# A memset in front of each gather of the first graph, and marks, reset rows and carried columns of the second graph moved from VectorE to ScalarE

## What is computed

```python
# first graph: 200,000 edges, sorted by dst
xn  = layernorm(x)
x   = x + relu(xn @ W + segment_sum((xn @ M)[src], dst))
# second graph: 131,072 edges, not sorted, plus one loop per node
h   = (xf @ W_gat).reshape(M, HEADS, NUM_EXPERTS)      # xf = layernorm(x)
e   = leaky_relu(a_src[src] + a_dst[dst], 0.2)
ee  = exp(e - segment_max(e, dst)[dst])
agg = segment_sum(h[src] * (ee / denom[dst])[:, :, None], dst)
scores = layernorm(agg).reshape(M, HEADS, NUM_EXPERTS).mean(1)
# two best experts per row, softmax weights w
out = sum over experts of  w[expert] * (gelu(xf @ W1 + b1) @ W2 + b2)
return x + out
```

## Time and profile before

| | |
|---|---|
| median of 3 runs | 3527.27 us (3522.12 to 3535.72) |
| the profiled execution | 3540.27 us |
| its span, first to last instruction | 3539.0 us |
| mean granted TensorE clock over the span | 0.882 |
| busy: TensorE / its weight loads | 2560.6 us (72%) / 1708.4 us (48%) |
| busy: VectorE | 2344.6 us (66%) |
| busy: ScalarE | 920.5 us (26%) |
| busy: POOL | 2377.0 us (67%) |
| mean DMA rate | 170 GB/s |

### The profile page before, as it was taken

How to read it: one execution, slowest core, us unless ns; L and a number is a source line. 1 busy time by engine, 2 the same in 40 slices (tenths; PEclk the granted TensorE clock), 3 DMA queues, 4 the chain that set the end, 5 groups by cost and what they waited for, 6 DMA issues and landing times.

```text
span 3539.0 us, 36336 instructions
## 1 busy us (share of the span) xinstructions
PE 2560.6 (72%) x10290; PEld 1708.4 (48%) x10315; DVE 2344.6 (66%) x5820; ACT 920.5 (26%) x1581; POOL 2377.0 (67%) x2827
## 2 busy tenths in 40 slices
PE   2556777767677777768877887777798787777725
PEld 1334555545555545546555555555554444443314
DVE  6677676776775555565545555555358898899957
ACT  3000111111112222211111111111145565555514
POOL 3666666666656666646666666666788888888841
PEclk9776998989888989889989888989799999999968
DMA  9676566666666666646666666666622122241147
GB/s 287 227 251 205 180 201 186 204 190 196 203 184 194 205 188 204 201 145 211 202 210 196 200 202 213 197 207 207 171 62 55 45 60 57 55 131 43 41 148 230
DMA packets 476775, 600.78 MB, mean 170 GB/s; under 512 B 72486, under 2 KB 415390, under 8 KB 474526
## 3 DMA queue, kind: packets, MB, share of 16 engines
q1 hardware_dynamic: 378766, 375.94, 32.9%
q0 software_dynamic: 97216, 219.88, 22.4%
q10 hardware_dynamic: 592, 2.64, 0.2%
HBM read 313.06 MB, written 286.79 MB: 169 GB/s over the span
## 4 chain that ended last, share of the span: by engine, by line
DVE 28%; PE 22%; another core or an unknown queue 12%; issue 9%; DMA 3%; ACT 2%; POOL 1%; SPq 0%; DVEq 0%; ACTq 0%; POOLq 0%
PE wide L1535 8%; DVE picked L901 6%; DVE g L905 6%; DVE ring L855 5%; PE wide L1585 4%; PE wide L1595 4%; PE wide L1645 3%; DVE one_hot L788 2%; DMA ring<-xn_d,srci 2%; PE wide L1554 1%; DVE by_row L996 1%; DVE by_row L1003 1%; POOL ring L1737 1%; DVE comb L1178 1%
## 5 line engine op out<-in xcount | busy, mean ns | idle before, releaser
L1737 POOL DMA_INDIRECT ring<-xn_d,srci x1611 | 1562.1, 970 | 907.6 <-issue 415.4
L855 DVE SCALAR_TENSOR_TENSOR ring<-ring,same_v,wide 128x256 f32<-128x256 f32 x1610 | 771.2, 479 | 930.7 <-remote 404.3
L1535 PE MATMUL wide<-ring,one_hot 128*128 128x256 f32 x3222 | 959.1, 435 | 381.8 <-DVE ring L855 194.1
L1535 PEld LDWEIGHTS wide<-ring,one_hot 128*128 128x128 f32 x3222 | 665.4, 216 | 632.0 <-issue 201.1
L1645 PE MATMUL wide<-tab_parts,low_hot 128*128 128x400 bf16 x3144 | 580.9, 339 | 144.6 <-DVE picked L901 102.6
L1789 POOL DMA_INDIRECT g<-tab_d,srt x500 | 496.0, 992 | 82.3 <-POOL pause L1746 49.8
L1645 PEld LDWEIGHTS wide<-tab_parts,low_hot 128*128 128x128 bf16 x3144 | 298.1, 99 | 422.2 <-issue 130.7
L1595 PE MATMUL wide<-w2s,hh 128*128 128x256 f32 x1568 | 413.5, 411 | 46.5 <-DVE yo L829 35.4
L1585 PE MATMUL wide<-xt,w1s 128*128 128x512 f32 (+1 forms) x832 | 420.3, 632 | 21.5 <-ACT hh L1264 13.9
L1264 ACT ACTIVATE hh<-wide,b1c 128x512 f32<-128x512 f32 (+1 forms) x208 | 137.6, 662 | 1000.5 <-PE wide L1585 404.3
L1595 PEld LDWEIGHTS wide<-w2s,hh 128*128 128x128 f32 x1568 | 325.5, 210 | 117.2 <-DVE yo L829 40.0
(11 more groups left out here) (369 smaller groups left out, 1778.0 us busy)
## 6 DMA issues: line engine op xcount, KB each, us to landing
run_d<-ring SPq DMA_DIRECT2D x201, 1024.0 KB
ring<-xn_d,srci POOLq DMA_INDIRECT x1611
y_d<-yo SPq DMA_DIRECT2D x196, 128.0 KB
comb<-y_d SPq DMA_DIRECT2D x28, 896.0 KB
low_row<-low_d SPq DMA_DIRECT2D x13, 1024.0 KB
sum_d<-g SPq DMA_DIRECT2D x15, 768.0 KB
g<-tab_d,srt POOLq DMA_INDIRECT x500
xn_d<-ring SPq DMA_DIRECT2D x7, 896.0 KB, 7.0
```

The costliest lines, as they stand in the source:

```text
L855: dve_at["run", j] = step(V.scalar_tensor_tensor(out=o, in0=ring[:, (j - 1) // JC % RING, (j - 1) % JC, :], scalar=same_v[:, j:j + 1], in1 ...
L1535: mm = T.matmul(bank[pair_bank[p]][:, j % 2 * D:(j % 2 + 1) * D], one_hot[:, j // 4 % 4, j % 4, :], ring[:, j // JC % RING, j % JC, :], st ...
L1737: G.indirect_dma_start(out=ring[:, s, j % JC, :], out_offset=None, in_=xn_d, in_offset=at_rows(srci[:, j:j + 1])).then_inc(sem(f"gather{s} ...
```

## The change

It has two independent parts. The first: `pause_once()`, until now defined further down and used in the second graph, is called in front of every gather of the first graph. The second: in the second graph, the mark of a segment's start is added to the exponent (`fade` gets -1e30 there and its exponential is 0), so the multiplication by `same_f` goes; the rows of `reset_c` for all chunks but the first are made by ScalarE, from `same_f` with a scale of 1e30 and a bias of -1e30; and the two column copies between chunks go to ScalarE. VectorE waits for them at the running maximum.

```diff
+    CARRY_COPIES = 2
+    far_below = r.take("far_below", [P, 1], F32)
+            step(V.memset(far_below[:, :], -BIG))
 # weigh(c), VectorE
-            step(V.tensor_scalar(reset_c[:, :, now], same_f[:, None, a:b].broadcast_to([P, HEADS, FC]), -1.0, BIG,
-                                 ALU.add, ALU.mult))
-            if c >= 1:
-                step(V.tensor_copy(logit[:, :, 0:1], rows_top[:, :, FC:FC + 1]))
+            if c == 0:
+                step(V.tensor_scalar(reset_c[:, :, now], same_f[:, None, a:b].broadcast_to([P, HEADS, FC]), -1.0, BIG,
+                                     ALU.add, ALU.mult))
...
             if c >= 1:
                 V.wait_ge(sem("rows_copied"), ROW_COPIES * c)
+                V.wait_ge(sem("carries"), CARRY_COPIES * c)
+                V.wait_ge(sem("resets"), c)
...
-            dve_at["weighed", c] = then(V.tensor_scalar(fade[:, :, now], fade[:, :, now], 0.0, None, ALU.min))
+            dve_at["weighed", c] = then(V.scalar_tensor_tensor(out=fade[:, :, now], in0=fade[:, :, now], scalar=0.0,
+                                                               in1=reset_c[:, :, now], op0=ALU.min, op1=ALU.add))
 # sum_up(c), VectorE
-            step(V.tensor_tensor(fade[:, :, now], fade[:, :, now],
-                                 same_f[:, None, a:b].broadcast_to([P, HEADS, FC]), ALU.mult))
...
-            if c + 1 < NCF:
-                then(V.tensor_copy(by_row[:, 0:FE, 0:1], by_row[:, 0:FE, FC:FC + 1]))
 # exps(c), ScalarE, behind the two exponentials
+            if c + 1 < NCF:
+                A.activation(reset_c[:, :, 1:FC + 1],
+                             same_f[:, None, (c + 1) * FC:(c + 2) * FC].broadcast_to([P, HEADS, FC]), ACT.Identity,
+                             bias=far_below[:, 0:1], scale=BIG).then_inc(sem("resets"), 1)
 # copy_rows(c), ScalarE, behind the copy of the maxima and behind the last copy
+            if c + 1 < NCF:
+                A.activation(logit[:, :, 0:1], by_row[:, FE:FG, FC:FC + 1], ACT.Copy).then_inc(sem("carries"), 1)
...
+            if c + 1 < NCF:
+                A.activation(by_row[:, 0:FE, 0:1], by_row[:, 0:FE, FC:FC + 1], ACT.Copy).then_inc(sem("carries"), 1)
 # POOL, the first graph's gathers
+        def pause_once():
+            n = next(pauses)
+            if n >= 2:
+                G.wait_ge(sem("paused"), n - 1)
+            G.memset(pause[:, :], 0.0).then_inc(sem("paused"), 1)
...
                 if j % 2 == 0 and j >= LEAD:
                     G.wait_ge(dve_step, dve_at["run", j - LEAD])
+                pause_once()
                 G.indirect_dma_start(out=ring[:, s, j % JC, :], out_offset=None, in_=xn_d,
                                      in_offset=at_rows(srci[:, j:j + 1])).then_inc(sem(f"gather{s}"), 16)
```

More of the change, by code:

```diff
@@ L1717, in gpsimd_program @@
                         pattern=[[1, P]], channel_multiplier=-1).then_inc(sem("consts_made"), 1)
+        pauses = itertools.count(1)
+        def pause_once():
[3 more added lines that the diff above has]
+            G.memset(pause[:, :], 0.0).then_inc(sem("paused"), 1)
         G.wait_ge(sem("pairs_out"), 80)
@@ L1736, in gpsimd_program @@
                     G.wait_ge(dve_step, dve_at["run", j - LEAD])
+                pause_once()
                 G.indirect_dma_start(out=ring[:, s, j % JC, :], out_offset=None, in_=xn_d,
                                      in_offset=at_rows(srci[:, j:j + 1])).then_inc(sem(f"gather{s}"), 16)
-        pauses = itertools.count(1)
-        def pause_once():
-            n = next(pauses)
-            if n >= 2:
-                G.wait_ge(sem("paused"), n - 1)
-            G.memset(pause[:, :], 0.0).then_inc(sem("paused"), 1)
         def starts(which):
```

## The result

| | runs | median us | lowest to highest |
|---|---|---|---|
| before | 6 | 3531.49 | 3519.52 to 3544.90 |
| after | 6 | 3510.63 | 3500.65 to 3537.54 |

The ratio is 0.994, 95% interval 0.9915 to 0.9965: the changed kernel is 21 us faster, 0.6%. I had forecast 3607 us, slower by 80.

What follows compares the result with a forecast made beforehand. The first graph (70% of the span) was taken as a loop of engines taking turns, none full, the second as VectorE's. +85 + 10 - 15 = +80 us on the 3527 us median gave 3607 us, range 3475 to 3690.

Steps and rivals of the forecast that it cites:

- The memset's price: First graph, POOL: a memset before each gather makes gather to gather 1.46 us instead of 1.25, 0.21 us each.
- A stall will no longer be made good, and TensorE will then wait for rows: First graph: POOL, almost never at leisure, can't catch up, so more gather groups reach TensorE late; +85 us.
- The rival of the even pace: First graph: evenly spaced gathers shorten unnamed waits at VectorE's sum and TensorE's visit by a third; 3477 us, chance 0.20.
- The rival in which the memset sits in POOL's waiting time: First graph: memsets fill POOL's 417 us of stalls, only the second graph gains 15 us; 3512 us, chance 0.17.
- The one-hots: First graph, VectorE: one-hot operations are held up by memsets they meet; +10 us, between nothing and +35 us.
- can hold up only one or two of them: First graph: one 0.35 us memset delays only one or two of four one-hots in a row, hence +10 us.
- ScalarE's work: Second graph: moving work to ScalarE takes 24.7 us of 718 off VectorE; -15 us, between 0 and -25.
- POOL leaves room: Second graph: POOL's last feature gather starts 23 us before VectorE uses the last chunk; supports the -15 us.
- The rival that ScalarE's work doesn't pay: Second graph: VectorE's 25 us become waits for TensorE, 15 us are missing; 3622 us, within the forecast's chance of 0.58.

Runs made afterwards that it cites:

- e7: Before, no memsets, first-graph gathers fetching half the bytes (results differ): first graph 2443.3 us, 49% of TensorE's recorded completions late; no time given.
- f2: Before, with half of each running sum's tiles stored a second time, no memsets in the first graph: 45% of completions late; no time given.
- e4: After, with an empty POOL instruction that each next gather waits for in place of the first graph's memsets: ratio to before 1.0174.
- e10: After, with 250 instead of 280 columns in the first graph's memsets: 29% of completions late at 1.442 us per gather; no ratio given.
- e12: After, with 220 columns in the first graph's memsets and gathers up to 22 ahead of the running sum instead of 14: first graph 2431.9 us.
- f1: After, without the memsets in front of the second graph's 500 gathers: 38 us above the changed kernel on the same chip.
- f5: After, with 220 columns in every memset, the second graph's too: ratio to before 1.0066.
- e1: Before, with the first graph's 1611 memsets alone, second graph unchanged: ratio to before 1.0022.
- e2: Before, with the second graph's part alone (work moved to ScalarE), no memsets in the first graph: ratio to before 0.9985.

## Why the prediction was wrong, step by step

**The memset's price was right.** 1611 memsets of 0.358 us; gather to gather 1.464 us, forecast 1.46.

**The step that failed** is "A stall will no longer be made good, and TensorE will then wait for rows", with the +85 us put on it. Its first half came true and more: TensorE's wait for rows rose from 139.7 to 479.2 us. But I added it to the stretch as if the rest stayed. The same spacing ended TensorE's late completions (47% to 13%), VectorE waited 146 us less in front of the running sum and POOL 396 us less for it, and the last gather came 23.5 us earlier in the profiled pair. On chip A the first graph takes 2441.2 us with memsets and 2443.0 without: the 0.21 us per gather bought back what they cost. The 15.8% of the chain that had no name were, for the most part, TensorE held up by POOL's gathers, and I left them as a constant.

**The rival of the even pace** had the right place, the unnamed waits, and 0.20. I set against it that "bytes and their mean rate don't change, and the stores are large whatever the gathers do". e7 and f2 show that neither bytes nor stores matter; the time between gathers does. Its price was wrong as well: it let a third of the unnamed waits go and still charged 95 us. Nearly all of them went, but named waits took their place, VectorE's for the visits and TensorE's for rows, so that 3510.6 us came out, not 3477. The rival in which the memset sits in POOL's waiting time gave 3512 us, close to the result by luck: it had the first graph's waits stay as they are.

**The one-hots.** I took +10 us, with +0.13 us each as the upper bound. They grew by exactly that, from 303 to 433 ns, and without memsets they take 301 ns in e4: it is the memset that does it. Its length matters, 307 ns with 16 columns, 351 with 220, 355 with 250, 433 with 280 and 473 with 420. The step that failed is that a memset "can hold up only one or two of them", four one-hots in a row. The Trainium skill ("SBUF — State Buffer", Who interferes with whom) says that the port pair is locked for the whole instruction, and I had read the upper bound as what that would give. The trace agrees in that the mean grew by the whole of that bound. What the growth costs in time no run measures by itself.

**ScalarE's work.** VectorE's busy time fell somewhat more than worked out (718 to 685.6 us, 693 forecast), but instead of -15 us the part gives 0.9985 of 3503 on chip A, some 5 us that are not clear of nothing, and 3.5 us over the 15 chunks. The step that failed is "POOL leaves room": I read it from the last chunk, and in most others VectorE waits for POOL's rows. The rival that ScalarE's work doesn't pay was nearly the case. The profiled pair shows no gain at all: there the 15 chunks take 697.7 us before (first L970 at 2685.7) and 714.2 after (first L972 at 2666.5). With the changed second graph they took 681.2 us in e10 and 728.9 in e12 on one chip, so a single pair can't tell 15 us there.

**Open.** By what the gathers hold TensorE up; why the loss of f1 and f5 lies ahead of the first chunk alone; whether it goes by the number of rows of a gather (not tried); why it begins nearer to 1.5 us on some chips than on others, and why e1 and e2 add up to 1.0007 on chip A while after has 0.9968 and 0.9974 on B and D.

## What to carry to other kernels

Before pricing a delay on one engine, look at what the waits without a name have in common: if they end when that engine pauses, the delay may pay for itself. A wait that loses its name is not yet time gained: look for it under the other names, and at the length of the stretch. In this kernel the pause between indirect gathers had a best length, since work was held up below it and POOL's pace was paid above: of the lengths tried it was 1.41 us per gather in the first graph on two chips (1.2% and 1.4%). The same length in the second graph lost time ahead of its first chunk. Such a length should be tried on several chips before it is kept.

## What the runs showed of the hardware

Trains of indirect gathers on POOL at 1.25 us each held TensorE up (45% to 49% of its recorded completions late, in one place 30 and 45 us without progress for the engines that wait), at 1.46 us hardly (0% on three chips, 7% and 13% on others). Steps of 1.25 and 1.75 us in turn held up nothing (0% in e4). The place of 30 and 45 us had the DMA engines at 0.20. By the Trainium skill ("SBUF — State Buffer", Who interferes with whom) TensorE waits on no other engine for SBUF's ports; if so, it is another resource that it shares with the gathers, and no run here names it.

One gather of after lasts 14.24 us, and it lies beside one operation of VectorE with two inputs:

```profile
1564.64 13.80 DVE L779 TENSOR_TENSOR high_hot<-iota_b,digit_f 128x13100 uint8<-128x13100 bf16 x1
1565.04 14.24 POOL L1755 DMA_INDIRECT ring<-xn_d,srci  x1 [0.16 <-POOL pause L1734]
```

The gather ends 0.84 us after that operation. The Trainium skill says in the same section that an operation of VectorE with two SBUF inputs contends with a GpSimd instruction that reads SBUF; the trace agrees, if the gather reads its row numbers there (`srci` is in its row). In before POOL was waiting for the running sum at that place, so nothing was lost by it there.
